# Residual and bias travel with the sent rows; results go straight into the output

## The reference

```
x = x + attention0(norm(x))            # 16 heads of 8 features
x = x + fp4_ffn(norm(x))               # hidden width 352, rows and weights rounded in blocks of 16
x = x + causal_rotary_attention(norm(x)) @ w_out.T + b_out
x = x + moe(norm(x)) + bias            # the step that the change touches

moe: scores = softmax(xn @ router)                 # 8 experts
     w, e = top_k(scores, 2)                       # first and second choice of a token
     for k in 0, 1:                                # each expert takes at most 512 tokens per choice
         y = gelu(xn[tokens of e] @ w1[e]) @ w2[e] # 128 -> 512 -> 128
         out[token] += y * w[:, k]                 # a token over the capacity gets nothing
```

## Time and profile before

| | |
|---|---|
| three timed runs | 1948.68 us median, 1946.59 to 1950.67 |
| the profiled execution: its own time, its span | 1966.64 us, 1964.9 us |
| PE, DVE, ACT, POOL busy | 84%, 60%, 74%, 12% of the span |
| `late_phase` | about 825 to 1809 us |
| `expert_phase` | 1809 to 1964.9 us |
| mean granted TensorE clock | 0.945 |

### The profile page before, as it was taken

How to read it: one execution, slowest core, us unless ns; L and a number is a source line. 1 busy time by engine, 2 the same in 40 slices (tenths; PEclk the granted TensorE clock), 3 DMA queues, 4 the chain that set the end, 5 groups by cost and what they waited for, 6 DMA issues and landing times. The chain is left out here.

```text
span 1964.9 us, 33364 instructions
## 1 busy us (share of the span) xinstructions
PE 1657.4 (84%) x12948; PEld 633.1 (32%) x12948; DVE 1185.5 (60%) x2109; ACT 1456.5 (74%) x2516; POOL 231.6 (12%) x255
## 2 busy tenths in 40 slices
PE   5489999999999999854889888889799888683994
PEld 3122222222222222232333333433243322221673
DVE  8899999999999996476354616453445333114112
ACT  4167777777878778614999999899999988791221
POOL 4400000000000000102000100010001032302454
PEclk9589999999999999977999999999999999996997
DMA  4300110000000000134111211122111311121233
GB/s 136 120 2 27 35 39 28 26 26 26 26 26 26 26 30 2 47 155 146 33 49 56 90 48 49 51 79 82 49 49 57 105 64 42 58 86 48 64 99 112
DMA packets 72078, 113.86 MB, mean 58 GB/s; under 512 B 9282, under 2 KB 58376, under 8 KB 66288
## 3 DMA queue, kind: packets, MB, share of 16 engines
q1 hardware_dynamic: 66672, 94.97, 15.4%
q0 software_dynamic: 5248, 16.75, 2.3%
HBM read 73.58 MB, written 37.95 MB: 57 GB/s over the span
## 5 line engine op out<-in xcount | busy, mean ns | idle before, releaser
L752 ACT ACTIVATE probs<-psS 128x512 f32<-128x512 f32 x1024 | 556.4, 596 | 187.6 <-PE psS L656 186.2
L771 DVE TENSOR_REDUCE max_of_halves<-psM 128x2 f32<-128x1024 f32 x512 | 617.6, 1222 | 46.5 <-PE psM L625 16.8
L1479 ACT ACTIVATE exps<-cpsS 128x1024 bf16<-128x1024 f32 x512 | 537.5, 1079 | 27.1 <-PE cpsS L1249 25.8
L1249 PE MATMUL cpsS<-rotary_stack 128*128 128x512 bf16 x1024 | 306.4, 388 | 72.6 <-ACT exps L1479 28.9
L676 PE MATMUL psO<-probs,plain_v 128*9 128x256 f32 x4096 | 316.9, 381 | 4.9 <-issue 2.3
L1489 ACT ACTIVATE cprobs<-cpsS 128x1024 f32<-128x1024 f32 x256 | 275.2, 1075 | 37.8 <-PE cpsO L1282 17.5
L1229 PE MATMUL cpsS<-rotary_stack 128*128 128x512 bf16 (+3 forms) x768 | 198.6, 335 | 72.5 <-ACT cprobs L1489 34.9
L625 PE MATMUL psM<-plain_top 64*128 64x512 bf16 x1024 | 212.2, 395 | 31.4 <-DVE max_of_halves L771 22.7
L656 PE MATMUL psS<-plain_top 64*128 64x512 bf16 x1024 | 213.2, 387 | 7.4 <-issue 6.1
L656 PE MATMUL psS<-plain_rest 64*128 64x512 bf16 x1024 | 207.6, 377 | 0.0
L1282 PE MATMUL cpsO<-cprobs,rotary_v 128*9 128x512 f32 (+3 forms) x1536 | 154.9, 491 | 0.6 <-DVE rotary_sums L1783 0.6
(11 more groups left out here) (283 smaller groups left out, 1635.5 us busy)
## 6 DMA issues: line engine op xcount, KB each, us to landing
rotary_stack<-q_parts SPq DMA_DIRECT2D x48, 192.0 KB
rotary_stack<-k_parts SPq DMA_DIRECT2D x48, 192.0 KB
rotary_stack<-q_rot_parts SPq DMA_DIRECT2D x48, 192.0 KB
rotary_stack<-k_rot_parts SPq DMA_DIRECT2D x48, 192.0 KB
plain_top<-q_parts SPq DMA_DIRECT2D x64, 96.0 KB
plain_top<-k_parts SPq DMA_DIRECT2D x64, 96.0 KB
tokens_taken<-sent_rows POOLq DMA_DIRECT2D x4, 1048.0 KB, 8.1
e_x<-tokens_taken SPq DMA_DIRECT2D x16, 262.0 KB, 4.2
```

The lines of the kernel that those rows point to most:

```text
L752: act.activation(pr[n % SLOTS_P][:, h, :], psS[u % RING][:, :], ACT.Exp, scale=SCALE).then_inc(s_e, 1)
L771: dve.tensor_reduce(mh[g % 2][:, :, hh, t, kh:kh + 1].rearrange("p e o -> p (e o)"), psM[n % 2][:, :, :], AX.X, ALU.max).then_inc(s_r, 1)
L1249: ins = pe.matmul(to[:, kh, :], q[:, x, y_ * P:(y_ + 1) * P], k[:, x, kh * CH:(kh + 1) * CH], start=True, stop=True)
L1479: act.activation(ex[d % EX][:, :, :], psS[n % 3][:, :, :], ACT.Exp, scale=SCALE, accum_out=den[:, at:at + 1]).then_inc(s_e, 1)
```

## The change

A sent row is now 259 f32 (`ROW` = 2 D + 3) and ends with 128 values of X plus the output bias. DVE makes these by the new task `base`, one for each half of a batch, and SP stores the same values to the output tensor, a half at a time. `send` holds three halves of a batch instead of two batches; `apply` of a half waits for the sends of the half three before it. The sends are ordered half by half, in fours (four tiles for the first choice, the same four for the second), and in batches 0 to 2 POOL waits before each further four until the four before have landed.

In `expert_phase` DVE adds the carried X plus bias to the weighted result of a first choice, and POOL scatters it into the output tensor; groups of second choices are loaded without the carried part and scattered with `compute_op=ALU.add`, after all first-choice scatters have landed. The tables `tokens_made`, the loads back, the adds to X, the stores of X and the one-instruction bias add are gone. The eight fills of `tokens_taken` are issued one after another.

```
-ROW = D + 3
+ROW = 2 * D + 3
+FILLS = 8
@@ what apply of a half needs besides @@
+def sent_tasks(b, c):
+    if 2 * b + c < 3:
+        return []
+    earlier, half = divmod(2 * b + c - 3, 2)
+    return [("send", earlier, 1, half * TC + TC - 1)]
...
+        for c in cs:
+            tasks.append((("base", b, c), "vector", 0.7, [("apply", b, "r", c), ("base", b, c - 1)], first))
...
-        last = earlier
-        for k, i in [(k, i) for k in range(2 if b < B - 1 else 1) for c in cs for i in range(c * TC, (c + 1) * TC)]:
-            tasks.append((("send", b, k, i), "other", 3.0 if b < B - 1 else 0.2, [last], first))
+        last = [earlier] + [("base", b, c) for c in cs]
+        for k, i in [(k, i) for c in cs for k in range(2 if b < B - 1 else 1) for i in range(c * TC, (c + 1) * TC)]:
+            tasks.append((("send", b, k, i), "other", 2.2 if b < B - 1 else 0.2, last, first))
...
+def sent_half(send, b, c):
+    return send[:, (2 * b + c) % 3, :, :]
...
+        def wait_sent(engine, n, cc):
+            if 2 * n + cc >= 3:
+                b, half = divmod(2 * n + cc - 3, 2)
+                for k in range(2):
+                    engine.wait_ge(s_sent[k][b % 2], 16 * (TB * (b // 2) + TC * (half + 1)))
...
@@ late_phase, DVE @@
+            def add_base(b, cc):
+                h = 2 * b + cc
+                dve.wait_ge(s_w, 16 * 5)
+                if h >= 3:
+                    dve.wait_ge(s_out[h % 3], 16 * (h // 3))
+                first = b * TB + cc * TC
+                dve.tensor_tensor(sent_half(send, b, cc)[:, :, WHO + 1:ROW], p.X[:, first:first + TC, :],
+                                  bias2[:, :].unsqueeze(1).broadcast_to([P, TC, D]), ALU.add).then_inc(s_base, 1)
...
                 elif kind == "send":
-                    if k == 0 and i == 0:
+                    if k == 0 and i % TC == 0:
+                        cc = i // TC
+                        wait_sent(pool, n, cc)
...
+                    if k == 0 and i % TC == 0:
+                        pool.wait_ge(s_base, base_at[n, i // TC] + 1)
+                    if n < B - 1 and i % TC == 0 and (k or i):
+                        pool.wait_ge(s_sent[1 - k][n % 2], 16 * (TB * (n // 2) + i + TC * k))
                     send_row(p, pool, send, slots, n, k, i, s_sent)
...
+            sp.dma_start(bias2[:, :], out_bias.rearrange("a b d -> (a b) d").broadcast_to([P, D])).then_inc(s_w, 16)
...
+                elif kind == "base":
+                    cc = label[2]
+                    sp.wait_ge(s_base, base_at[n, cc] + 1)
+                    sp.dma_start(out[n, cc * CH:(cc + 1) * CH, :].rearrange("(t p) d -> p t d", p=P),
+                                 sent_half(send, n, cc)[:, :, WHO + 1:ROW]).then_inc(s_out[(2 * n + cc) % 3], 16)
...
@@ expert_phase, POOL @@
+            rows = out.rearrange("b n d -> (b n) d")
+            for i in range(3):
+                pool.wait_ge(s_out[i], 16 * ((2 * B - 1 - i) // 3 + 1))
             for s in range(NS):
+                if s == E:
+                    for i in range(KEPT):
+                        pool.wait_ge(s_sc[i], ROWS * (E // KEPT))
                 pool.wait_ge(s_yk, s + 1)
...
+                    to = bass.IndirectOffsetOnAxis(ap=who[:, t, :], axis=0)
+                    if s < E:
+                        pool.indirect_dma_start(rows, to, ye[s % KEPT][:, t, :], None, bounds_check=TOK - 1, oob_is_err=False
+                                                ).then_inc(s_sc[s % KEPT], 16)
+                    else:
+                        pool.indirect_dma_start(rows, to, ye[s % KEPT][:, t, :], None, bounds_check=TOK - 1, oob_is_err=False,
+                                                compute_op=ALU.add).then_inc(s_sc[s % KEPT], 16)
+            for i in range(KEPT):
+                pool.wait_ge(s_sc[i], ROWS * (NS // KEPT))
...
@@ expert_phase, SP, tokens @@
+                wide = ROW if s < E else WHO + 1
...
@@ expert_phase, DVE, keep_y @@
+                if s < E:
+                    ins.then_inc(s_yg, 1)
+                    dve.wait_ge(s_yg, s + 1)
+                    ins = dve.tensor_tensor(ye[s % KEPT][:, :, :], ye[s % KEPT][:, :, :], xe[s % LOADS][:, :, WHO + 1:ROW], ALU.add)
+                ins.then_inc(s_yk, 1)
...
-                if s >= NS - B:
-                    add(0, s - (NS - B))
-            for b in range(B):
-                add(1, b)
```

More of the change, by code:

```diff
@@ L1042, in choice_tasks @@
         for c in cs:
[L1043 removed]
+            tasks.append((("apply", b, "r", c), "vector", 1.4, [norm] + sent_tasks(b, c), first))
         for c in cs:
@@ L1311, in fill @@
                         t = label[2] * TC + i
-                        rows = send[:, n % 2, t, 0:D] if kind == "rt" else xn[:, t, :]
+                        rows = sent_half(send, n, t // TC)[:, t % TC, 0:D] if kind == "rt" else xn[:, t, :]
                         ins = pe.transpose(to[:, i * P:(i + 1) * P], rows, p.ident[:, :])
@@ L1527, in apply @@
                 if kind == "r" and n == 0:
[L1528 to L1531, removed]
+                    dve.wait_ge(s_zs, 16 * FILLS)
+                if kind == "r":
+                    wait_sent(dve, n, cc)
                 if kind == "p":
@@ L1536, in apply @@
                 for i in range(cc * TC, (cc + 1) * TC):
-                    to = send[:, n % 2, i, 0:D] if kind == "r" else xn[:, i, :]
+                    to = sent_half(send, n, cc)[:, i % TC, 0:D] if kind == "r" else xn[:, i, :]
                     ins = dve.tensor_scalar(to, p.X[:, n * TB + i, :], mv[:, i, 0:1], rstd[:, i:i + 1], ALU.subtract, ALU.mult)
@@ L1668, in choose @@
                 dve.wait_ge(s_d, ch.n)
-                ch.inc(dve.tensor_copy(send[:, b % 2, tiles, D:WHO], best[:, tiles, 0:2]))
+                for c in range(tiles.start // TC, tiles.stop // TC):
+                    ch.inc(dve.tensor_copy(sent_half(send, b, c)[:, :, D:WHO], best[:, c * TC:(c + 1) * TC, 0:2]))
                 ch.link(dve.tensor_copy(whichf[:, :, tiles], which[:, tiles, 0:2].rearrange("p t k -> p k t")))
@@ L1818, in _ @@
             pool.wait_ge(s_zm, 1)
[L1819 to L1825, removed]
+            pool.memset(send[:, :, :, WHO:WHO + 1], 1.0e9).then_inc(s_zm, 1)
             pool.wait_ge(s_zm, 2)
-            rows = p.taken.rearrange("(a p b) d -> a p (b d)", a=4, p=P)
-            for i in range(4):
+            rows = p.taken.rearrange("(a p b) d -> a p (b d)", a=FILLS, p=P)
+            for i in range(FILLS):
                 pool.dma_start(rows[i, :, :], zeros).then_inc(s_zs, 16)
@@ L1936, in _ @@
                 work(label)
+            for _, label in plans[2]:
+                work(label)
 class ExpertWeights:
@@ L1961, in down, with expert_phase @@
         return self.w[e // self.half][:, e % self.half, f, :]
-def expert_phase(p, send, slots, experts, s_sent, bias, out):
+def expert_phase(p, send, slots, experts, s_sent, s_out, out):
     nc = p.nc
```

74 lines of the change are left out of this document (23 added, 51 removed).

## The result

The changed kernel took 1942.29 us (median of 10 executions, 1941.24 to 1944.97), the kernel before 1948.58 us beside it (10, 1946.59 to 1950.67): ratio 0.9966, interval 0.9957 to 0.9975. So it is faster, by 6.3 us where 20.3 were forecast, and the time is 0.3 us above the range's upper end of 1942.

The account below looks back on a forecast made before the run. ACT was taken to bound the late phase, PE the expert phase, with its head and tail exposed. Terms -11.7 (tail net of adding scatters), -1.1, +0.45 and -8.0 gave -20.3 us: 1948.68 to 1928.4, range 1915 to 1942.

Parts of the forecast that it names:

- what stands behind the last scatter's issue: End of expert phase: loads back, add and store go, nothing follows the last scatter; -15.7 us, 0.8 more for landing.
- adding scatters ahead of it: POOL, expert phase: adding scatters 1.67 us apart instead of 1.27, only the last eight count; +3.2 us.
- head: Expert phase before PE's big matmuls: bias load and add go, row loads take longer; 1.1 us gained.
- start of the late phase: One more load before the weights' count that PE waits for; its issue on SP costs +0.45 us.
- sends in fours: Late phase, batches 0 to 2: shorter send runs remove half of ACT's 16.1 us of pauses; -8.0 us.
- rest of the late phase: DVE's eight base adds (5.5 us in all), SP's eight stores and waits for landed sends are covered; 0 us.
- rival 1: Late phase: pacing the sends gives nothing, pauses absent from timed runs or otherwise caused; 1936.3 us, chance 0.27.
- The span ends within about 4 us of the last scatter's issue: Sign at the kernel's end: span closes that soon, with no load back and no store of X behind it.
- the point of no gain: Expert phase: adding scatters at 2.2 us each, POOL busy 1.9 us in place of 0.97, leave no gain.
- the limit for PE to stay the bound: Expert phase sign: while an adding scatter's own duration is under 1.55 us, PE stays the bound.
- The wait at group 8: Expert phase: POOL waits for first choices' scatters, loses 0.6 us against 2.3 us slack a group; cost nothing.
- Rival 4: Late phase: sends land late (over 4.2 us), DVE holds PE and ACT in three batches; 1948 us, chance 0.08.

Follow-up runs that it names:

- second profile: The kernel before, unchanged, profiled once more: 1948.4 us beside 1948.79, ratio 0.9996.
- eights: Changed kernel with a half batch's sends in one run of eight instead of two of four: 1941.66 us beside 1948.79; again, 1954.16 us beside 1970.82.

## Why the prediction was wrong

Faster was right, and so were most mechanisms; the size was out by a factor of three. The terms, for the quiet chip (the kernel before has there, in its second profile, the same 17.0 us behind the last scatter's issue and 139.1 us from the first load to it as in its first):

| step | forecast | measured |
|---|---|---|
| what stands behind the last scatter's issue (-15.7 and 0.8 for the landing) | -14.9 | -8.8 (17.0 to 8.2 us) |
| adding scatters ahead of it | +3.2 | +3.8 |
| head | -1.1 | -3.4 |
| start of the late phase | +0.45 | +3.5 |
| sends in fours | -8.0 | 0 |
| rest of the late phase | 0 | -1.4 (what is left over; no cause shown) |
| sum | -20.3 | -6.3 |

- **Sends in fours: the largest miss, 8 us.** "I take half, -8.0 us" split the difference between two worlds that both exist; on neither chip is half the answer. The sign that the prediction itself gave, a profiled execution of 1966.64 us against a median of 1948.68, was the pauses' full price. Read on its own it said that the timed runs had none, and then rival 1 (1936.3) had been the likelier, itself still 6 us under the measured 1942.29. The mechanism (a run of sends too long makes ACT pause) held on the other sort of chip, with -18.4 us. By the rule of the Trainium skill ("DMA: Bandwidth & Descriptors", section "Queues, rings and completion order") fours would give nothing: the quiet chip agrees with 0 us, the other with its 18.4 us doesn't.
- **Tail: "After the change nothing follows the last scatter" is the step that failed in the trace, by 6 us.** Nothing in the kernel follows, but POOL needs 5.4 to 6.2 us from its last work until the program, or the next phase, goes on. Before the change the loads back, the add and the store covered it: 1947.89 + 6.2 = 1954 lies well before 1964.9. It could have been read: POOL's timeline has the same 6.26 us at the border between the two phases, before the change too. "The span ends within about 4 us of the last scatter's issue" was the sign asked for, and the 8.2 us of the trace speak against it.
- **Start: right place, wrong size.** The forecast took the issue on SP (0.45 us) for the load's price. What counts is its landing, 5.3 us behind the issue, on a count that PE already waited for.
- **Adding scatters: right.** They are 1.85 us apart where 1.67 was taken, only the last eight count, as the prediction said, and they cost 3.8 us where 3.2 was taken (0.57 us each where 0.4 was taken, 4.6 in all, less what two slow plain ones of before had cost). That is under the point of no gain (2.2), and the busy time of 1.54 us is just under the 1.55 that was named as the limit for PE to stay the bound. The wait at group 8 was put at nothing: 0.6 us late, against a slack of 2.3 us a group. That slack is the plain scatters'; by the prediction's own 1.67 it was 0.7, and measured it is 0.06. So the lateness stays to the end: 0.3 us on the quiet chip, 1.7 to 2.2 on the others, where the difference of the kinds grew to 6.85 us by it.
- **Head: right, and too small.** The loads were slower, as foreseen (9.6 us in place of 4.2 in the median), but PE's first turn came sooner: 3.6 us behind the first issue of a load of rows (1792.87 to 1796.49) in place of 4.5 (1809.55 to 1814.08). That the bias load of before had shared their time is likely and wasn't tried.
- **Rival 4** did not happen: ACT's waits show no hold by landed sends, and none of DVE's in the same stretch is for a transfer.

## What to carry to other kernels

When a tail is taken away, ask what it was hiding: look for the same engine's last instruction elsewhere in the trace, at another phase's border, and put its way out into the sum. A load added to a count that an engine already waits for costs its landing, not its issue; put it behind the loads that are urgent, on a count of its own. An idle time in front of an instruction isn't yet the price of the wait that ended it: ask when the instruction could have started without it (here 0.3 us of 2.19). When a profiled execution is longer than the timed ones by as much as a set of pauses, the pauses aren't in the timed runs: make that the forecast rather than half of it, and measure on more than one chip.

## What the runs showed that was not expected

- POOL's way out of a phase: 5.4 to 6.2 us of silence after its last work or wait, with a send of its own under way or without, at the border and at the end (6.2 with the final wait moved to SP); 0.3 us at the border when POOL had left before. Other engines can do their work beside it.
- The same program pauses in some comparisons, each on a chip of its own, and not in others: 1948.4 us and 1969.4 us, steady within 0.4% in each, with 9 to 16 indirect sends in a row. The pauses go with fours (18.4 us gained) and for the greater part with eights. What the pausing engines lack isn't shown.
- A scatter of 128 rows that adds costs POOL 1.54 us in place of 0.97; the transfer's rate while they stand alone is 33 to 37 GB/s.
- Of two loads of the same kind, one row of 512 bytes for all 128 partitions, issued 0.9 us apart, one landed in 2.3 us (`l_bias`) and the other in 5.3 (`l_out_bias`); 262 KB of rows take 4.2 us.
